# Causal mask of a 16-head self-attention: block rows inside the K=32 products and small triangle products, in place of 128x128 mask products

## Chip, cores, metric

The kernel runs on one core of a Trainium2 chip (trn2). The metric is the device time of one execution in microseconds (us).

## What is computed

A decoder of two layers over x of shape 64 x 128 x 128 (batch, position, model). The change touches only the first sublayer, a causal self-attention with 16 heads of width 8:

```python
x = x + _L0_attn_ref(_layernorm(x), W_dq, W_uq, W_dkv, W_uk, W_uv, W_o)

Q = ((x @ W_dq) @ W_uq).reshape(B, S, 16, 8)      # K, V alike
scores = jnp.einsum('bqhd,bkhd->bhqk', Q, K) / math.sqrt(8)
scores = jnp.where(causal, scores, -jnp.inf)
attn = jax.nn.softmax(scores, axis=-1)
out = jnp.einsum('bhqk,bkhd->bqhd', attn, V).reshape(B, S, 128)
return out @ W_o
```

Behind it come a cross-attention, a sparse mixture of 8 experts, a second self-attention, a second cross-attention and a dense mixture of 4 experts.

## The kernel before

The stage `self_attention` (L283 and on) works on one batch of 128 positions per step. It is software-pipelined by hand: in slot t every engine does, in a fixed order, its part of step t minus a lag (TURN, PROJECT, SCORE, SHIFT, WEIGH, VALUE, LAST, ADD). `run_slots` writes slots 0 to 23 and 64 to 83 out in full and runs slots 24 to 63 as a loop of 8 slots a turn, so it jumps back four times. Engines are tied by semaphores alone; each engine's order is the order of the code.

The 16 heads are 4 groups `g` of 4 heads. A group's 32 rows of `q` and of the block-diagonal `k_bd` lie in partitions 32g to 32g+31 (`strip(g)`), so a product of a group uses 32 rows of TensorE (K=32), and four groups can run side by side. Each group has a PSUM bank `ps_s[g]` of 128 x 512 (4 heads x 128). The groups form two pairs, (0, 1) and (2, 3).

Each batch's scores are made twice. First natural, queries in partitions (SCORE, products at L366): DVE takes each row's negated maximum over the keys (L547, two operations a pair, semaphore `max_done`). Then it splits those maxima in three bf16 parts (`pad`, L581 to L586), TensorE transposes `pad` (L399), and DVE spreads it to `m_bd` (L565, `shift_ready`). Two slots after SCORE they are made again turned, keys in partitions (WEIGH, products at L371), in the same banks, with the negated maxima added by a K=32 product of ones with `m_bd` (L357); ACT takes the exponentials (L445, `exp_done`), TensorE multiplies them by the values (VALUE, L390), and so on.

TensorE's slot is: `half(sl, 0)` (natural scores of pair 0, turned scores of pair 1), VALUE, two transposes (L399, L405), `half(sl, 1)` (natural of pair 1, turned of pair 0), then L413, the projections L420 to L422, L427 and L433. A half begins with the mask: a 128-row product of a bf16 identity with a 128 x 128 table of 0 and -1e30, over 512 columns, for each of its four banks (`masked`, L333): the natural ones wait for `exp_done`, the turned ones for `max_done`, one wait per bank:

```python
for n, g in enumerate(PAIRS[other]):
    pe.wait_ge(max_done[other], 2 * upto(sl, s + 2 + pair) - 1 + n)
    ...
    masked(ps_s[g], c.mask_k)
pe.wait_ge(shift_ready, s + 1)
```

DVE's slot is: statistics L557, maxima of pair 0 (L547), `m_bd` (L565), the residual (L571), maxima of pair 1 (L547), the split into `pad` (L581 to L586), L591, L596, L602. ACT's: exponentials of pair 1, L456, L461, L466, exponentials of pair 0, then `kT` (L476), q, v, xT. POOL builds `k_bd` from `kT` (L524) and small norm scalars. SP loads the tables (L267) and later streams zeros to memory.

## Time and profile before

| | |
|---|---|
| median of 3 runs | 3181.57 us (3179.53 to 3188.43) |
| the profiled execution's own time | 3173.24 us |
| its span | 3171.5 us |
| mean granted TensorE clock in it | 0.958 |
| this stage in the span | about 20 to 509 us |

The profiled execution is one run with its own time, 8.3 us under the median. PE is the matmul side of TensorE, PEld its weight loads, which overlap PE. A releaser is the instruction whose semaphore ended an idle time; "issue" means that nothing shown was waited for.

### The profile page before, as it was taken

The numbers are of one execution on the slowest core, as the hardware profiler recorded it, in microseconds if no ns is written. First come the engines' busy times: TensorE is split into PE (matmuls) and PEld (weight loads), VectorE is DVE, ScalarE is ACT, GpSimd is POOL, SyncE is SP. The second block draws the span as 40 slices with busy tenths as digits, with TensorE's granted clock in tenths as the row PEclk, the third lists the DMA queues.
The fourth block names the chain that finished last, engine by engine and source line by source line (L and its number), as shares of the span: only waits on it lengthen the run. The fifth ranks groups of instructions, "written<-read, shape, count | busy, mean of one in ns | idle before, by whom it ended". The sixth has DMA issues, their size and how long they took to land. (4 is left out here: it accounts for less than half of the span.)

```text
span 3171.5 us, 79074 instructions
## 1 busy us (share of the span) xinstructions
PE 2810.4 (89%) x26182; PEld 2315.9 (73%) x26183; DVE 2213.5 (70%) x4747; ACT 1914.9 (60%) x4303; POOL 1819.8 (57%) x2990
## 2 busy tenths in 40 slices
PE   6999997999999999499995999996789999999996
PEld 4666675888888888387774777774467777777775
DVE  4877885667666676445553999996878787878643
ACT  2555553666666666354442667674677777777762
POOL 3333333556666666425556777773667777777752
PEclk9999998999999999699997999997699999999998
DMA  5555563000000000122222000000000000000000
GB/s 151 156 143 157 157 169 107 2 5 13 14 11 13 13 12 15 68 69 74 74 74 68 1 0 0 0 0 1 1 1 5 8 5 8 5 8 5 8 5 10
DMA packets 205118, 129.51 MB, mean 41 GB/s; under 512 B 14256, under 2 KB 197528, under 8 KB 204184
## 3 DMA queue, kind: packets, MB, share of 16 engines
q1 hardware_dynamic: 196632, 108.60, 12.1%
q0 software_dynamic: 8192, 16.79, 1.7%
q8 instruction: 208, 3.41, 0.4%
q14 instruction: 86, 0.70, 0.1%
HBM read 34.85 MB, written 90.51 MB: 40 GB/s over the span
## 5 line engine op out<-in xcount | busy, mean ns | idle before, releaser
L445 ACT ACTIVATE a_e<-a_ps_s 128x512 f32<-128x512 f32 x256 | 138.9, 595 | 216.9 <-PE a_ps_s L371 216.9
L1575 POOL TENSOR_TENSOR a_qk<-a_qkv 128x2048 f32<-128x2048 f32 x64 | 235.3, 3676 | 57.8 <-ACT a_qkv L1550 53.6
L1508 PE MATMUL a_ps_s<-a_qk,w_ident 128*128 128x256 f32 x1024 | 236.7, 385 | 26.5 <-POOL a_qk L1575 26.4
L988 POOL TENSOR_TENSOR x_p<-x_p,x_rz 128x1232 f32<-128x1232 f32 x64 | 143.9, 2248 | 170.4 <-DVE x_rz L1097 170.4
L1508 PEld LDWEIGHTS a_ps_s<-a_qk,w_ident 128*128 128x128 f32 x1024 | 192.1, 192 | 55.9 <-issue 22.4
L524 POOL TENSOR_TENSOR a_k_bd<-a_kT,w_block 128x512 f32<-128x512 f32 x64 | 67.1, 1050 | 280.2 <-ACT a_kT L476 280.2
L1366 POOL DMA_INDIRECT f_yg<-f_rows_out,f_index x128 | 122.8, 959 | 177.7 <-DVE f_yo L1446 159.3
L547 DVE TENSOR_REDUCE a_nmax<-a_ps_s 128x4 f32<-128x512 f32 x256 | 164.0, 682 | 84.3 <-PE a_ps_s L366 84.3
L1557 ACT ACTIVATE a_r<-a_o,w_a_rows 128x128 f32<-128x128 f32 x512 | 220.8, 522 | 2.1 <-DVE a_o L1607 2.1
L2224 POOL TENSOR_TENSOR x_sq<-x_e 128x1232 f32<-128x1232 f32 x64 | 143.3, 2240 | 127.4 <-DVE x_t_sq L2383 127.3
L1104 DVE TENSOR_REDUCE x_top<-x_ps_s 128x16 f32<-128x1232 f32 x64 | 91.2, 1425 | 110.3 <-PE x_ps_s L728 110.3
L2102 ACT ACTIVATE x_pT<-x_ps_s 77x512 f32<-77x512 f32 x256 | 142.3, 590 | 34.6 <-PE x_ps_s L1979 34.6
L1526 PEld LDWEIGHTS a_ps_y<-w_a_o,a_r 128*128 128x128 f32 x1024 | 123.1, 195 | 54.6 <-issue 36.3
L865 ACT ACTIVATE x_uu_hi<-x_ps_u 128x308 fp32r<-128x308 f32 x256 | 101.7, 423 | 90.6 <-PE x_ps_u L728 90.4
L366 PE MATMUL a_ps_s<-a_k_bd,a_q 32*128 32x128 f32 x2048 | 154.1, 289 | 1.2 <-issue 1.2
L2205 POOL TENSOR_TENSOR x_d<-x_d,x_g 128x1232 f32<-128x1232 f32 x64 | 144.0, 2249 | 18.5 <-ACT x_g L2164 18.5
L1526 PE MATMUL a_ps_y<-w_a_o,a_r 128*128 128x128 f32 x1024 | 131.4, 283 | 24.4 <-DVE x L1622 24.2
L1979 PE MATMUL x_ps_s<-w_ident,x_d 128*77 128x128 f32 x1024 | 145.2, 280 | 7.7 <-DVE x_d L2366 7.6
L1597 DVE TENSOR_TENSOR a_ev<-a_ps_e,a_qkv 128x2048 f32<-128x2048 f32 x64 | 146.0, 2281 | 5.2 <-ACT a_ps_e L1564 4.1
L882 ACT ACTIVATE x_pT<-x_ps_s 77x512 f32<-77x512 f32 x256 | 140.0, 594 | 13.4 <-PE x_ps_s L786 12.0
L1979 PEld LDWEIGHTS x_ps_s<-w_ident,x_d 128*77 128x77 f32 x1024 | 124.4, 152 | 31.2 <-issue 22.1
L1019 POOL DMA_INDIRECT f_rows_in<-f_xr,f_where x120 | 121.1, 1009 | 39.2 <-issue 28.6
(588 smaller groups left out, 9755.6 us busy)
## 6 DMA issues: line engine op xcount, KB each, us to landing
f_rows_in<-a_zeros SPq DMA_DIRECT2D x31, 1088.0 KB, 5.4
f_rows_out<-a_zeros SPq DMA_DIRECT2D x31, 1088.0 KB, 10.2
f_xin<-f_rows_in SPq DMA_DIRECT2D x135, 64.0 KB
f_rows_out<-f_yo SPq DMA_DIRECT2D x135, 64.0 KB
out<-x SPq DMA_DIRECT2D x16, 256.0 KB
f_raw<-in_late_f SPq DMA_DIRECT2D x2, 1408.0 KB, 6.1
w_ctx<-in_ctx SPq DMA_DIRECT2D x1, 2464.0 KB
f_rows_in<-f_xr,f_where POOLq DMA_INDIRECT x128
```

Source lines behind the costliest of these rows:

```text
L366: nat = nc.tensor.matmul(ps_s[g][:, j * P:j * P + P], q[strip(g), u % 4, :], k_bd[strip(g), u % 4, j, :], start=False, stop=j == GROUP - 1)
L547: nc.vector.tensor_reduce(nmax[:, g, :], ps_s[g][:, :].rearrange("p (t k) -> p t k", t=GROUP), AX.X, ALU.max, negate=True).then_inc(max_do ...
L988: nc.gpsimd.tensor_tensor(wide, wide, rz[:, :].unsqueeze(2).broadcast_to([P, HEADS, K]), ALU.mult).then_inc(p_ready, 1)
L1508: ins = nc.tensor.matmul(ps_s[u % 2][:, 0:HEADS * HEADS], c.ident[:, :], qk[:, u % 2, k, :, :], start=k == 0, stop=k == HD - 1)
L1526: ins = nc.tensor.matmul(ps_y[:, 0:D], r[:, u % 2, k, :, :], c.w["a1_o"][:, k, :], start=k == 0, stop=k == HD - 1)
L1557: ins = nc.scalar.activation(r[:, u % 2, :, :, a], o[:, u % 2, :, :].rearrange("p h d -> p d h"), ACT.Copy, scale=c.w["a1_rows"][:, a:a + 1])
L1575: nc.gpsimd.tensor_tensor(qk[:, u % 2, :, :, :], qkv[:, u, 0, :, :].unsqueeze(3).broadcast_to(full), qkv[:, u, 1, :, :].unsqueeze(2).broad ...
L1597: nc.vector.tensor_tensor(ev[:, :, :, :], weights_of(u).unsqueeze(2).broadcast_to(n), qkv[:, u, 2, :, :].unsqueeze(1).broadcast_to(n), ALU ...
L1979: ins = nc.tensor.transpose(ps_s[0:K, r, j * P:j * P + P], d[:, spread % RING, r, j, :], c.ident[:, :])
L2102: nc.scalar.activation(pT[:, GROUP * r:GROUP * r + GROUP, :], ps_s[0:K, r, :].rearrange("p (j q) -> p j q", j=GROUP), ACT.Copy).then_inc(p ...
L2205: nc.gpsimd.tensor_tensor(wide, wide, g[:, a, b, :].unsqueeze(2).broadcast_to([P, HEADS, K]), ALU.mult).then_inc(dg_ready, 1)
L2224: nc.gpsimd.tensor_tensor(sq[:, :, :], e[:, s % 2, :, :], e[:, s % 2, :, :], ALU.mult).then_inc(sq_ready, 1)
```

## The change

The mask is written as products of 32 rows. Positions are cut in four blocks of 32. A whole block of later keys is masked by block rows: three rows of a strip hold a block indicator on one side and -1e30 for earlier blocks on the other. For the natural scores that is an own K=32 product per bank (`coarse_q`, `coarse_k`, new L348) over 512 columns, which now opens the bank. For the turned scores the same rows ride inside the shift product (`shift16` and rows of `pad` that the split never writes; `a0_block` lets them through in L565), which now opens the bank. The four diagonal blocks are masked by `causal_tiles` (new L334): per bank four K=32 products, `place16` (a shifted 32-row identity) with a 32 x 32 triangle repeated over 4 heads, 128 columns each. A half has four banks, so sixteen of them. The waits become one per pair: for the second operation of `exp_done` and of `max_done`; `shift_ready` is waited for ahead of `max_done`. The tables come as one load of 128 x 10 x 128 bf16 (320 KB) in place of four of 32 KB, and `a0_block` is a further load of 2 KB. DVE's one-time memset of `pad` becomes a copy.

```diff
--- before.py
+++ after.py
@@ -329,9 +329,10 @@
 
         @block.tensor
         def _(pe):
-            def masked(bank, mask):
-                nc.tensor.matmul(bank[:, :].rearrange("p (t k) -> p t k", t=GROUP), c.ident16[:, :],
-                                 mask[:, :].unsqueeze(1).broadcast_to([P, GROUP, P]), start=True, stop=False)
+            def causal_tiles(g, tri, n):
+
+                nc.tensor.matmul(ps_s[g].rearrange("p (t k) -> p t k", t=GROUP)[:, :, n * STRIP:n * STRIP + STRIP], c.place16[strip(g), n, :],
+                                 tri[strip(g), :].unsqueeze(1).broadcast_to([STRIP, GROUP, STRIP]), start=False, stop=False)
 
             def half(sl, pair):
 
@@ -339,22 +340,28 @@
                 scored, weighed = sl.step(SCORE), sl.step(WEIGH)
                 if scored:
                     s, u = scored
-                    for n, g in enumerate(PAIRS[pair]):
-                        if sl.fixed and s < 3 - pair:
-                            wait(pe, max_done[pair], 2 * s - 1 + n)
-                        else:
-                            pe.wait_ge(exp_done[pair], 2 * (s - 2 + pair) - 1 + n)
-                        masked(ps_s[g], c.mask_q)
+                    if sl.fixed and s < 3 - pair:
+                        wait(pe, max_done[pair], 2 * s)
+                    else:
+                        pe.wait_ge(exp_done[pair], 2 * (s - 2 + pair))
+                    for g in PAIRS[pair]:
+                        nc.tensor.matmul(ps_s[g][:, :].rearrange("p (t k) -> p t k", t=GROUP), c.coarse_q[strip(g), :],
+                                         c.coarse_k[strip(g), :].unsqueeze(1).broadcast_to([STRIP, GROUP, P]), start=True, stop=False)
                 if weighed:
                     s, u = weighed
-                    for n, g in enumerate(PAIRS[other]):
-                        pe.wait_ge(max_done[other], 2 * upto(sl, s + 2 + pair) - 1 + n)
-                        if sl.fixed and s + 2 + pair > B:
-                            pe.wait_ge(exp_done[other], 2 * s - 1 + n)
-                        masked(ps_s[g], c.mask_k)
                     pe.wait_ge(shift_ready, s + 1)
+                    pe.wait_ge(max_done[other], 2 * upto(sl, s + 2 + pair))
+                    if sl.fixed and s + 2 + pair > B:
+                        pe.wait_ge(exp_done[other], 2 * s)
                     for g in PAIRS[other]:
-                        nc.tensor.matmul(ps_s[g][:, :], c.ones16[strip(g), :], m_bd[strip(g), u % 2, :, :], start=False, stop=False)
+                        nc.tensor.matmul(ps_s[g][:, :], c.shift16[strip(g), :], m_bd[strip(g), u % 2, :, :], start=True, stop=False)
+                for n in range(GROUPS):
+                    if scored:
+                        for g in PAIRS[pair]:
+                            causal_tiles(g, c.tri_q, n)
+                    if weighed:
+                        for g in PAIRS[other]:
+                            causal_tiles(g, c.tri_k, n)
                 if scored:
                     s, u = scored
                     pe.wait_ge(q_ready, s + 1)
@@ -538,7 +545,7 @@
 
         @block.vector
         def _(dve):
-            nc.vector.memset(pad[:, :, :, :], 0.0)
+            nc.vector.tensor_copy(pad[:, :, :, :], c.a0_pad.rearrange("p (h r) -> p h r", r=HD).unsqueeze(1).broadcast_to([P, 2, HEADS, HD]))
 
             def maxima(at, pair):
                 s, u = at
@@ -563,7 +570,7 @@
                     wait(dve, sT_ps[0], s - 1)
                     wait(dve, sT_ps[1], s - 1)
                     nc.vector.tensor_tensor(m_bd[:, u % 2, :, :], ps_pad.unsqueeze(1).broadcast_to([P, GROUP, P]),
-                                            c.block[:, 0:GROUP].unsqueeze(2).broadcast_to([P, GROUP, P]),
+                                            c.a0_block[:, 0:GROUP].unsqueeze(2).broadcast_to([P, GROUP, P]),
                                             ALU.mult).then_inc(shift_ready, 1)
                 if at := sl.step(ADD):
                     s, u = at
@@ -2571,9 +2578,11 @@
                 c.w[name] = sb("w_" + name, shape, inp[name].dtype, life)
                 tiles[name] = c.w[name][(slice(None),) * len(shape)]
         keep = [(name, tiles[name]) for name in inp if name in tiles]
-        c.ident, c.ident16, c.ones_row = c.w["ident"], c.w["a0_ident16"], c.w["ones_row"]
-        c.mask_q, c.mask_k, c.ones16 = c.w["a0_mask_q"], c.w["a0_mask_k"], c.w["a0_ones16"]
-        c.block = c.w["block"]
+        c.ident, c.ones_row = c.w["ident"], c.w["ones_row"]
+        c.ident16, c.a0_pad, c.shift16, c.coarse_q, c.coarse_k = (c.w["a0_rows16"][:, n, :] for n in range(5))
+        c.place16 = c.w["a0_rows16"][:, 5:9, :]
+        c.tri_q, c.tri_k = (c.w["a0_rows16"][:, 9, n * STRIP:n * STRIP + STRIP] for n in range(2))
+        c.block, c.a0_block = c.w["block"], c.w["a0_block"]
         c.keys = inp["ctx"].shape[2]
         c.ctx = c.w["ctx"]
         c.rest = whole.enter_context(nc.semaphore("rest"))
@@ -2632,12 +2641,21 @@
     r = np.arange(P)
     strip = r % STRIP
     block = (strip[:, None] // HD == np.arange(GROUP)).astype(np.float32)
-    later = np.where(r[None, :] > r[:, None], MASKED, 0.0)
+    behind = strip - 2
+    coarse = (strip[:, None] == np.arange(3, 3 + GROUPS - 1)).any(axis=1)
+    low = MASKED * (r[None, :] // STRIP < behind[:, None]) * coarse[:, None]
+    at = (r[None, :] // STRIP == behind[:, None]) * coarse[:, None]
+    pad = np.zeros((P, GROUPS, GROUP, HD))
+    pad[:, :, 0, 3:3 + GROUPS - 1] = low[3:3 + GROUPS - 1].T[:, None, :]
+    place = [(strip[:, None] == r[None, :] - STRIP * n) for n in range(GROUPS)]
+    tri = np.zeros((P, P))
+    tri[:, 0:STRIP] = MASKED * (np.arange(STRIP)[None, :] > strip[:, None])
+    tri[:, STRIP:2 * STRIP] = MASKED * (strip[:, None] > np.arange(STRIP)[None, :])
+    rows = [np.eye(P), pad.reshape(P, P), (strip % HD < 3)[:, None] * ~coarse[:, None] + at, low, at] + place + [tri]
     return {
-        "ident": np.eye(P, dtype=np.float32), "a0_ident16": np.eye(P).astype(bf),
-        "a0_mask_q": later.astype(bf), "a0_mask_k": later.T.astype(bf), "a0_ones16": np.ones((P, P)).astype(bf),
+        "ident": np.eye(P, dtype=np.float32), "a0_rows16": np.stack(rows, axis=1).astype(bf),
         "tri4": triangles(4),
-        "block": block,
+        "block": block, "a0_block": np.maximum(block, coarse[:, None]).astype(np.float32),
         "ones_row": np.ones((1, P), np.float32),
     }
```

TensorE, the start of the second half of a slot (behind the transpose of `o`), before. A wait is named in brackets.

```order
L405 MATMUL a_ps_qkv<-w_ident,a_o 128x128 [waits a0_oT_ready,a0_v_ready,a0_o_ready]
L333 MATMUL a_ps_s<-w_a_mask_q,w_a_ident 128x512 [waits a0_exp_done1] x2
L333 MATMUL a_ps_s<-w_a_mask_k,w_a_ident 128x512 [waits a0_max_done0] x2
L357 MATMUL a_ps_s<-a_m_bd,w_a_ones 128x512 [waits a0_shift_ready]
L357 MATMUL a_ps_s<-a_m_bd,w_a_ones 128x512
L366 MATMUL a_ps_s<-a_k_bd,a_q 128x128 [waits a0_bd_ready,a0_q_ready]
L366 MATMUL a_ps_s<-a_k_bd,a_q 128x128
L371 MATMUL a_ps_s<-a_q,a_k_bd 128x128 x2
```

And in the changed kernel (`w_a_rows` is the new table):

```order
L412 MATMUL a_ps_qkv<-w_ident,a_o 128x128 [waits a0_oT_ready,a0_v_ready,a0_o_ready]
L348 MATMUL a_ps_s<-w_a_rows 128x512 [waits a0_exp_done1]
L348 MATMUL a_ps_s<-w_a_rows 128x512
L357 MATMUL a_ps_s<-a_m_bd,w_a_rows 128x512 [waits a0_max_done0,a0_shift_ready]
L357 MATMUL a_ps_s<-a_m_bd,w_a_rows 128x512
L334 MATMUL a_ps_s<-w_a_rows 128x4x32 x16
L373 MATMUL a_ps_s<-a_k_bd,a_q 128x128 [waits a0_bd_ready,a0_q_ready]
L373 MATMUL a_ps_s<-a_k_bd,a_q 128x128
L378 MATMUL a_ps_s<-a_q,a_k_bd 128x128 x2
```

Four 128-row products with their own waits are gone; the two openers of the natural banks, the two shift products and sixteen products of 128 columns stand ahead of the same L366 and L371 (now L373 and L378). The wait for `max_done` now stands at the shift product, beside `shift_ready`.

SP, the first loads, before:

```order
L265 DMA x<-in_x 128x4x128
L267 DMA w_ident<-in_ident 128x128
L267 DMA w_a_ident<-in_a_ident 128x128
L267 DMA w_a_mask_q<-in_a_mask_q 128x128
L267 DMA w_a_mask_k<-in_a_mask_k 128x128
L267 DMA w_a_ones<-in_a_ones 128x128
L267 DMA w_tri<-in_tri 128x32
L267 DMA w_block<-in_block 128x4
```

and in the changed kernel:

```order
L265 DMA x<-in_x 128x4x128
L267 DMA w_ident<-in_ident 128x128
L267 DMA w_a_rows<-in_a_rows 128x1280
L267 DMA w_tri<-in_tri 128x32
L267 DMA w_block<-in_block 128x4
L267 DMA w_a_block<-in_a_block 128x4
L267 DMA w_ones_row<-in_ones_row 1x128
```

Four loads became one, and `a_block` is new: two fewer ahead of the rest.

## Rows read from the trace of the kernel before

**Rows 1.** Page, part 1: busy time of each engine, whole span.

```profile
PE 2810.4 (89%) x26182; PEld 2315.9 (73%) x26183; DVE 2213.5 (70%) x4747; ACT 1914.9 (60%) x4303; POOL 1819.8 (57%) x2990
```

**Rows 2.** Stretches: from:to, length, busy (instructions) per engine, PE clock, DMA share, GB/s.

```profile
400.00:500.00 100.00, 99.49 (x1752) 72.24 (x1748) 82.64 (x222) 53.05 (x151) 32.33 (x72) 1.00 0.62 172
216.00:228.00 12.00, 11.54 (x153) 7.82 (x154) 5.04 (x12) 4.11 (x11) 3.73 (x15) 0.72 0.35 98
```

**Rows 3.** Waits of the stage, 36 to 506 us: in total, times, longest.

```profile
DVE a_nmax L547 <- PE a_ps_s L366: 84.3, 69, 15.9
...
PEld a_ps_s L333 <- DVE a_nmax L547: 25.9, 60, 0.5
```

**Rows 4.** Timeline of DVE, one slot: start, us, what, count, [idle before it, releaser].

```profile
299.09 1.29 DVE L547 TENSOR_REDUCE a_nmax<-a_ps_s 128x4 f32<-128x512 f32 x2 [0.80 <-PE a_ps_s L366]
...
300.94 0.93 DVE L581 CAST a_pad<-a_rest 128x16 bf16<-128x16 f32 x1
...
303.16 1.27 DVE L547 TENSOR_REDUCE a_nmax<-a_ps_s 128x4 f32<-128x512 f32 x2
...
306.03 1.29 DVE L547 TENSOR_REDUCE a_nmax<-a_ps_s 128x4 f32<-128x512 f32 x2 [0.80 <-PE a_ps_s L366]
```

**Rows 5.** Timeline of PEld (weight loads), second half of the slot.

```profile
304.49 0.10 PEld L333 LDWEIGHTS a_ps_s<-w_a_mask_k,w_a_ident 128*128 128x128 bf16 x1 [0.45 <-DVE a_nmax L547]
304.81 0.09 PEld L357 LDWEIGHTS a_ps_s<-a_m_bd,w_a_ones 32*128 32x128 bf16 x2 [0.23 <-issue]
304.82 0.19 PEld L366 LDWEIGHTS a_ps_s<-a_k_bd,a_q 32*128 32x128 f32 x2
```

**Rows 6.** Timeline of PE, second half of the slot.

```profile
304.81 0.39 PE L357 MATMUL a_ps_s<-a_m_bd,w_a_ones 32*128 32x512 bf16 x2
...
305.04 0.27 PE L371 MATMUL a_ps_s<-a_q,a_k_bd 32*128 32x128 f32 x2
...
305.70 0.27 PE L366 MATMUL a_ps_s<-a_k_bd,a_q 32*128 32x128 f32 x1
...
305.71 0.38 PE L371 MATMUL a_ps_s<-a_q,a_k_bd 32*128 32x128 f32 x3
```

**Rows 7.** Timeline of ACT, then POOL, around the DVE row at 300.94.

```profile
299.21 1.08 ACT L445 ACTIVATE a_e<-a_ps_s 128x512 f32<-128x512 f32 x2 [1.48 <-PE a_ps_s L371]
300.23 0.28 ACT L476 ACTIVATE a_kT<-a_ps_qkv 128x128 f32<-128x128 f32 x1
...
300.73 1.08 POOL L524 TENSOR_TENSOR a_k_bd<-a_kT,w_block 128x512 f32<-128x512 f32 x1 [5.03 <-ACT a_kT L476]
```

**Rows 8.** Timeline of DVE, last scored slot, where no a_k_bd is built.

```profile
497.35 0.20 DVE L581 CAST a_pad<-a_rest 128x16 bf16<-128x16 f32 x1
```

**Rows 9.** Timeline of PE, small products of another stage.

```profile
686.12 0.23 PE L851 MATMUL x_ps_misc<-x_mask,w_x_all 128*128 128x32 bf16 x3
686.20 0.24 PE L854 MATMUL x_ps_misc<-x_mask,w_x_all 128*128 128x8 bf16 x4
```

**Rows 10.** Timeline, another stage: a DVE operation and the load behind a separate wait.

```profile
527.34 0.48 DVE L1035 TENSOR_TENSOR x_uu_lo<-x_ps_u,x_uu_hi 128x308 fp32r<-128x308 f32 x1 [4.41 <-ACT x_uu_hi L865]
...
527.94 0.29 PEld L726 LDWEIGHTS x_ps_u<-x_keys_hi,x_a_hi 128*128 128x128 f32 x1 [0.78 <-issue]
```

**Rows 11.** Timeline of PEld, DVE and PE at loop turns.

```profile
155.79 0.13 PEld L333 LDWEIGHTS a_ps_s<-w_a_mask_q,w_a_ident 128*128 128x128 bf16 x2 [2.90 <-issue]
...
159.36 0.69 DVE L547 TENSOR_REDUCE a_nmax<-a_ps_s 128x4 f32<-128x512 f32 x1 [3.12 <-PE a_ps_s L366]
...
218.13 0.42 PE L366 MATMUL a_ps_s<-a_k_bd,a_q 32*128 32x128 f32 x1
219.00 0.36 PE L366 MATMUL a_ps_s<-a_k_bd,a_q 32*128 32x128 f32 x1 [0.46 <-issue]
```

**Rows 12.** Timeline of SP's queue (SPq) at the start.

```profile
2.22 0.43 SPq L267 DMA_DIRECT2D w_a_mask_q<-in_a_mask_q  x1
2.70 0.43 SPq L267 DMA_DIRECT2D w_a_mask_k<-in_a_mask_k  x1
```

## Prediction

> **What bounds the kernel now.** I read five views. The page gives PE 2810.4 us of a 3171.5 us span [rows 1], which would make TensorE the bound. The change, though, lies in one stage of some 490 us, so the stretch table comes next: from 400 to 500 us PE is busy 99.49 of 100, DVE 82.64 [rows 2]. A busy PE is a modelled one, so this doesn't say what a shorter TensorE slot would be worth. The waits of the stage do: DVE waits 84.3 us for the natural scores (L366), 69 times, and TensorE's load waits 25.9 us, 60 times, for DVE's maxima [rows 3]. Each waits for the other once a slot: a loop between two engines, and its length is the slot.
>
> The timeline shows it. DVE's maxima of pair 1 start at 299.09 and again at 306.03, so the slot is 6.94 us, with one idle time of 0.80 in it [rows 4]. All the rest DVE works or is held. The maxima of pair 0 end at 303.16 + 1.27 = 304.43 [rows 4]. Call this time T. At 304.49 TensorE's load of the last mask product of the second half is released; the load of the shift product follows at 304.81 [rows 5]; the last natural product ends at 305.70 + 0.27 = 305.98 [rows 6], and DVE goes on at 306.03 [rows 4]. So T to DVE's next start is 1.60 us, and this is TensorE's only share in the loop. The rest of its slot is ahead of T or behind 306, beside DVE's work.
>
> A second branch of the loop: the last turned product ends at 305.71 + 0.38 = 306.09 [rows 6]. The slot before shows what hangs on it: exponentials at 299.21 for 1.08, `kT` at 300.23, and POOL's `k_bd` from 300.73 for 1.08 [rows 7]. DVE's cast at 300.94 takes 0.93 us [rows 4], where the same cast takes 0.20 without a `k_bd` beside it [rows 8]; it ends as `k_bd` ends (301.87 and 301.81). So DVE's small operations are held to the end of `k_bd`, which goes back to the last turned product. That product is the one that sets the slot: natural scores a little earlier or later meet the same hold.
>
> **What TensorE saves, and where it lies.** A product of 512 bf16 columns holds its strip for about 0.22 us (L357 at 304.81, L371 of its strips at 305.04 [rows 6]). A half loses four full-array mask products in series, 4 x 0.22 = 0.87. The two natural openers use other strips than the shift products and run beside them: nothing added. The sixteen triangles are four per strip, strips side by side, 128 columns or 0.055 each: 4 x 0.055 = 0.22. Behind them the first fp32 load of a strip is exposed: an fp32 load takes 0.19 and a bf16 one 0.09 [rows 5], so it streams about 0.10, of which the last triangle hides 0.055: 0.05. Saved are 0.87 - 0.27 = 0.60 a half, 1.2 a slot, some 75 us of TensorE's time in 63 slots. It lies ahead of T: TensorE comes to the second half's shift product over 1 us sooner and waits there for DVE.
>
> **What changes behind T.** Removed: from 304.49 to 304.81, one mask product and the change from 128-row to 32-row products: -0.33 [rows 5]. The change of form isn't gone but made earlier, by the natural openers. Added: the triangles, 0.22, and the exposed load, 0.05, since both now stand behind `max_done`, and nothing of them can run ahead of it. Also the wait itself. Until now `max_done` was on the weight load: 0.06 from DVE's end to the load (304.43, 304.49). Now L357 has two waits and the first in the code is `shift_ready`; the second becomes an instruction of its own. Another stage prices that: DVE ends at 527.34 + 0.48 = 527.82 and the load starts at 527.94, 0.12 [rows 10]: +0.06. Behind it queue the triangles and all L373 and L378, for which DVE and ACT wait. Sum for the turned branch: -0.33 + 0.22 + 0.05 + 0.06 = 0.00; I take +0.02 for the gaps of a few ns between triangles, times 60 slots: **+1 us**.
>
> The bounds of this term. The triangles' spacing in four strips is not in this trace. Below: four fp32 products start within 0.01 to 0.02 us and the next four 0.11 later, so strips hardly hinder each other; with triangles fully packed and the load hidden it is -0.05 a slot, -3 us. Above: the small products at 686.12 start 0.025 to 0.027 apart (three from 686.12, the next at 686.20) although 32 columns need half of that [rows 9]. At 0.025 each sixteen take 0.40: +0.18 a slot, +11 us, more if DVE meets `k_bd` an operation earlier. Those are whole-array loads, one behind the other, and mine are in four strips, so I stand near the first end.
>
> The Trainium skill speaks against this change here: "TensorEngine Tiling (Array Packing)", section Instruction Overhead, says that each matmul costs some 60 cycles whatever its width and warns of small ones, which is 0.025 us. The rows of the products of 8 and 32 columns agree with it; by that rule the sixteen would cost 0.40 and the sum would be 3191, not 3180.
>
> **First half of a slot.** It needs the maxima of pair 1 and saves 0.60 too, but DVE is then in its small operations and comes to the natural scores of pair 0 only at 303.16 [rows 4], when they have long been there (no idle time stands at that row). Nothing gained. The `exp_done` wait for both operations of a pair costs nothing: at 299.21 + 1.08 = 300.29 they are done [rows 7], before TensorE gets there.
>
> **Loop turns.** Four times the loop jumps back, TensorE's loads pause 2.90 us and DVE idles 3.12 [rows 11]. There TensorE is late, so its first half is on the path and shorter masks can give 0.6 to 1.3 each. But some 70 instructions behind the jump it pauses again in two of the four turns (218.13 to 219.00, "issue" [rows 11]), as if instructions came late; the new half has 28 more (14 loads, 14 products), uses them up faster, and has more left behind that pause: up to +1 each. Between -5 and +4 us, I take **-2**.
>
> **Start and end.** Two fewer loads are issued ahead of the others, 0.47 apart (2.22, 2.70 [rows 12]); 200 KB more are moved. Between -1 and +1, I take **-0.5**. `a0_block` for `block` in L565 has the same shape: 0. The copy for a memset on `pad` is once, beside POOL's start: 0. The later stages are the same work: 0.
>
> **Sum.** 1 - 2 - 0.5 = -1.5 us. Against the profiled execution's own 3173.24 (span 3171.5) that is 3171.7. Its time is 8.3 under the median of the runs, 3181.57, which stands for the kernel: 3181.57 - 1.5 = **3180 us**. A difference of 0.3%, 9.5 us, is about what a measurement of this kernel tells from none.
>
> **Rivals.**
> - *Small products too dense (slower).* The triangles go 0.025 apart. Turned scores then end 0.18 later a slot, natural ones, whose loads queue behind all sixteen, up to 0.2 later, so that the hold by `k_bd` catches DVE one small operation sooner (0.24 more). It decides from 0.16 a slot on (9.5 / 60). For: [rows 9]. Against: the starts of four strips within 0.02. Time: +11 to +25, 3193 to 3206, say 3197. Chance 0.17.
> - *TensorE slows for its new idle time (slower).* It idles over 1 us a slot in one piece. From 216 to 228, behind the pause at a turn, the granted clock is 0.72 [rows 2], so partly at 1.2 GHz instead of 2.4. At 1.2 the 1.5 us behind T double; ten such slots more are +15, 3196. Against: from 400 to 500 the clock is 1.00 [rows 2] although loads wait up to 0.45 a slot for DVE [rows 5]. Chance 0.07.
> - *TensorE is the bound after all (faster).* If the natural scores came sooner by all that TensorE saves, DVE's idle 0.80 would go: 60 x 0.8 = 48 us, 3133. For: PE at 99%. Against: what DVE waits for is released by DVE itself 1.60 us before. Chance 0.05.
> - *The loop gets a little shorter (faster).* Strips independent, all four turns at their best, DVE's small operations fall better around `k_bd`: -0.1 to -0.2 a slot and -5, so -11 to -17, 3168. Chance 0.11.
>
> **How the numbers follow.** The forecast, within 9.5 us of before, keeps 0.60. Faster is 0.05 + 0.11 = 0.16, slower 0.17 + 0.07 = 0.24. The range leaves out the bound case (0.05) and the upper parts of the two slower ones (about 0.1): 3167 to 3199.
>
> **What would show it.** After the change: the slot stays at 6.9 to 7.0 us. DVE's idle time ahead of the maxima of pair 1 stays near 0.8 (0.7 to 0.8 if strips are independent, 1.0 if products are 0.025 apart). PE's busy time in the stage falls, and the load of L357 waits about 1 us a slot for DVE (L554), where 25.9 us stood in all before. DVE's operation beside `k_bd` still takes 0.93. Starts of L334 in one strip stand 0.055 to 0.06 apart. The forecast is wrong if DVE's idle time shrinks below 0.5, if `k_bd` no longer meets DVE's small operations, or if the clock of the stage falls under 0.9.

## The result and the profile after

The changed kernel takes 3215.35 us (median of 4 runs, 3205.61 to 3220.97), the kernel before 3180.55 in the same session (4 runs, 3176.11 to 3188.43): a ratio of 1.0103, 95% interval [1.0071, 1.0136]. It is slower by 1%, where 3180 and no change were forecast. The profiled execution of the kernel after is the fastest of its four (3205.61 us), so what the two traces below account for is a difference of 32.3 us of span (3171.5 and 3203.8), not the 34.8 of the medians.

Page, part 1, of the kernel after (span 3203.8 us), against [rows 1]; then its stretches of [rows 2] and one of the later x0 stage, with the same columns:

```profile
PE 2786.1 (87%) x27974; PEld 2342.9 (73%) x27975; DVE 2218.4 (69%) x4747; ACT 1921.6 (60%) x4303; POOL 1818.8 (57%) x2990
```

```profile
400.00:500.00 100.00, 89.95 (x2091) 73.46 (x2091) 80.58 (x210) 52.72 (x150) 32.83 (x71) 0.97 0.57 158
850.00:950.00 100.00, 94.23 (x815) 84.09 (x815) 65.13 (x137) 61.96 (x133) 63.30 (x105) 0.98 0.03 12
```

TensorE runs 1792 products more and is busy less. In the stretch it falls from 99.49 to 89.95 of 100, and the whole didn't get faster by it. The slot itself is what was forecast. Timeline of DVE, one slot of the kernel after:

```profile
299.84 1.27 DVE L554 TENSOR_REDUCE a_nmax<-a_ps_s 128x4 f32<-128x512 f32 x2
...
302.61 1.29 DVE L554 TENSOR_REDUCE a_nmax<-a_ps_s 128x4 f32<-128x512 f32 x2 [0.71 <-PE a_ps_s L373]
...
304.46 0.94 DVE L588 CAST a_pad<-a_rest 128x16 bf16<-128x16 f32 x1
...
306.69 1.27 DVE L554 TENSOR_REDUCE a_nmax<-a_ps_s 128x4 f32<-128x512 f32 x2
...
309.46 0.69 DVE L554 TENSOR_REDUCE a_nmax<-a_ps_s 128x4 f32<-128x512 f32 x1 [0.71 <-PE a_ps_s L373]
```

The slot is 309.46 - 302.61 = 6.85 us (6.94 before), the idle time 0.71 (0.80), and the cast beside `k_bd` still takes 0.94. Over slots 7 to 60 of both traces the undisturbed ones (up to 8% over the median) have a mean of 6.91 us, against 6.97 before. TensorE's saved time stands as waiting ahead of its shift product. Loads of the same slot, then the waits of the stage (36 to 506 us: in total, times, longest), against [rows 3]:

```profile
301.16 0.09 PEld L357 LDWEIGHTS a_ps_s<-a_m_bd,w_a_rows 32*128 32x128 bf16 x2 [0.88 <-DVE a_nmax L554]
```

```profile
DVE a_nmax L554 <- PE a_ps_s L373: 89.3, 72, 13.0
PEld a_ps_s L357 <- DVE a_nmax L554: 33.1, 36, 1.1
...
PEld a_ps_s L348 <- issue: 17.2, 10, 4.5
...
PE a_ps_s L348 <- issue: 14.7, 4, 4.2
...
PEld a_ps_s L378 <- issue: 7.0, 4, 2.3
PE a_ps_s L378 <- issue: 5.4, 3, 2.1
```

The rows that matter are those "<- issue": TensorE waits for nothing that the profile shows, in a few long pieces. Before, the largest were 13.1 us in 10 (L333). By stage, from the first instruction on a tile of each (before, after): a0 from the first `a_ps_s` to the first `x_bank` 477.6 and 491.0 us (+13.4); then wide_weights and x0 to the first `f_w_hi` 809.9 and 827.4 (+17.5), though that code is unchanged; the rest +1.5. The x0 stage loses it at one place of its loop, which jumps back four times. Timeline of PE behind one of these jumps (a branch at 967.69):

```profile
971.87 0.40 PE L733 MATMUL x_ps_s<-x_uu_hi,x_x_hi 128*128 128x308 f32 x1 [1.59 <-issue]
972.11 0.31 PE L734 MATMUL x_ps_s<-x_uu_lo,x_x_hi 128*128 128x308 f32 x1
972.25 0.31 PE L735 MATMUL x_ps_s<-x_uu_hi,x_x_lo 128*128 128x308 f32 x1
974.35 0.62 PE L733 MATMUL x_ps_s<-x_uu_hi,x_x_hi 128*128 128x308 f32 x1 [1.79 <-issue]
```

There is a pause at the jump, three products, and a second pause. The kernel before has the first kind alone (1.58 us ahead of the product at 861.30, at its first x0 jump).

The second pause is 2.0 to 2.3 us without a weight load, 8.7 us in the four turns, about half of what the stage lost. The other half is TensorE's clock behind it. One pass of the loop, from branch to branch, in the kernel before, in the kernel after, and in x0_shifted_12 (below), where the second pause is gone, with the columns of [rows 2]:

```profile
951.80:1046.50 94.70, 90.61 (x803) 80.75 (x802) 64.82 (x136) 60.55 (x131) 61.51 (x105) 1.00 0.03 13
```

```profile
967.70:1066.60 98.90, 93.28 (x803) 83.18 (x801) 64.97 (x136) 61.12 (x131) 61.48 (x105) 0.97 0.03 12
```

```profile
959.80:1053.70 93.90, 90.55 (x802) 80.67 (x801) 64.86 (x136) 60.92 (x131) 61.64 (x105) 1.00 0.03 11
```

The same 803 products keep PE busy for 93.28 us in place of 90.61. Over the four passes that is 9.8 us more of busy time in 16.4 us more of length (395.0 for 378.6), and the trace of the kernel after has 23.8 us of them at half the clock (1.2 GHz), each stretch beginning in a second pause or just over 1 us behind it. The kernel before and x0_shifted_12 have none there.

**What the pauses have in common.** I numbered the instructions of TensorE's program (a product is two, load and product; a wait of its own is one) and put them beside the trace. All pauses of this second kind stand at numbers that leave the same rest when divided by 256, up to ten instructions. In the a0 stage of the kernel after TensorE stops 9 behind number 1758, 9 and 3 behind 4830 (in the first and the last pass of the loop), and 10 behind 6110, 6878 and 9182, and in the x0 stage at 14046; each of these is 222 + a multiple of 256. The page counts 223 transfers of the instruction queue (208 before), and each one of them in the trace is 16384 bytes, which is 256 instructions of 64 bytes. From 400 to 510 us, in straight code, there are 19 of them for 18 blocks of 256 instructions of TensorE. I call 222 + 256n an **edge**. The x0 loop starts 60 instructions ahead of an edge in the kernel before and 11 ahead of one in the kernel after, because TensorE's program in front of it has grown by 1841 instructions, which is 7 x 256 + 49.

The Trainium skill says this in "Runtime: NRT & Kernel Launch", section Instruction fetch mechanics: instructions come in 16 KiB blocks of 256, fetched one after the other ahead of use, and a taken branch out of the blocks held forces a fetch before work goes on. The trace agrees with both. The section also calls the crossing of a block's end mostly hidden; the trace shows up to 2.4 us there.

### The profile page after: what moved, and what is told of

Its sections match the earlier page's. It is cut to its first block and busy times, and to the rows that moved or that the text cites. A ratio compares the mean times of both kernels' runs of the same rounds, so it can differ in the third digit from the quotient of the medians.

```text
span 3203.8 us, 82733 instructions
## 1 busy us (share of the span) xinstructions
PE 2786.1 (87%) x27974; PEld 2342.9 (73%) x27975; DVE 2218.4 (69%) x4747; ACT 1921.6 (60%) x4303; POOL 1818.8 (57%) x2990
## 5 line engine op out<-in xcount | busy, mean ns | idle before, releaser
L373 PE MATMUL a_ps_s<-a_k_bd,a_q 32*128 32x128 f32 x2048 | 156.2, 293 | 1.8 <-issue 1.8
L378 PE MATMUL a_ps_s<-a_q,a_k_bd 32*128 32x128 f32 x2048 | 151.2, 286 | 5.4 <-issue 5.4
L1533 PE MATMUL a_ps_y<-w_a_o,a_r 128*128 128x128 f32 x1024 | 131.6, 283 | 24.2 <-DVE x L1629 23.7
```

The source lines that it names most:

```text
L373: nat = nc.tensor.matmul(ps_s[g][:, j * P:j * P + P], q[strip(g), u % 4, :], k_bd[strip(g), u % 4, j, :], start=False, stop=j == GROUP - 1)
L378: turned = nc.tensor.matmul(ps_s[g][:, j * P:j * P + P], k_bd[strip(g), u % 4, j, :], q[strip(g), u % 4, :], start=False, stop=j == GROUP - 1)
L1533: ins = nc.tensor.matmul(ps_y[:, 0:D], r[:, u % 2, k, :, :], c.w["a1_o"][:, k, :], start=k == 0, stop=k == HD - 1)
```

## Experiments

Sessions on the chip differ: the kernel before took 3180.6, 3146.6, 3148.5, 3146.2 and 3182.7 us in the five groups of runs below, most of it in the experts' stage (859 to 866 us from `f_w_hi` to `f1w`, or 836 to 839, whatever the kernel). The x0 stage differs too: 797.8 us in hybrid_masks and 807.6 in hybrid_max_first, for the same x0 code. So ratios to the kernel before of the same group are compared, and stage times of the traces. Theory A: instructions come late. Rival B: chance, or the clock. Rival D: triangles and waits behind `max_done`. "Excess" is the time of slots 7 to 60 over the same number of median slots. Some expectations count the x0 stage from 13 us earlier: their 823 and 840 us are the 809.9 and 827.4 here.

### Is it the place of the code?

x0_shifted_back. Tiny products move the x0 loop of the kernel after to 59 instructions ahead of an edge:

```diff
+            for n in range(104):
+                nc.tensor.matmul(spare[:, 0:8], c.ident16[:, :], c.ident16[:, 0:8], start=True, stop=True)
```

> The changed kernel with 104 tiny products (8 columns, into an unused bank; 208 instructions) at the end of TensorE's part of wide_weights, where TensorE waits for other engines. The x0 loop then starts in TensorE's program 8 x 256 instructions behind its place before the change, up to one instruction. Theory A (instructions arrive in pieces of 256, and the loss of the later stage comes from where its loop lies against the edges of the pieces): the second pause behind each of the four jumps of the x0 loop (2.1 to 2.4 us, L735 to L733) goes, the x0 stage (first bank product to the first f_w_hi operation) falls from 840.4 to about 823 us, and the median falls from 3215 to about 3198. The a0 stage stays 13 us longer than before the change. Rival B (the x0 loss is chance or the clock's doing): the stage stays at 840 and the pauses stay. Rival C (the added products cost time): the stage gets 3 us longer.

1.0052 [1.0036, 1.0069], x0 stage 813.0 us. The second pauses are gone. The a0 stage, the same code, is 497.3 us (491.0 in the trace of after, 486.8 in that of x0_shifted_12 below), so a0 varies by some 10 us between executions. Rival B falls as the first cause, since the pauses go with the place of the code; the added products cost nothing that shows.

x0_shifted_before. The same with `range(24)` in the kernel before:

> The kernel before with 24 such tiny products (48 instructions) at the same place: the x0 loop starts 12 instructions ahead of an edge of 256, as in the changed kernel, instead of 60. Theory A: a second pause of 2.1 to 2.4 us comes behind each of the four jumps of the x0 loop, the stage grows from 823 to about 839 us, the median from 3181 to about 3196. Rival B (chance or clock): stage 823, median 3181 within 9. Nothing of the change itself is in this kernel, so a slower time can't be due to masks.

1.0060 [1.0043, 1.0077], x0 stage 827.0 (809.9), 20.4 us of its four passes at half the clock. 48 instructions that nothing needs make the kernel before 0.6% slower, by the mechanism forecast. Timeline of PE behind a jump (branch at 961.60), where the kernel before has one pause:

```profile
966.02 0.40 PE L729 MATMUL x_ps_s<-x_uu_hi,x_x_hi 128*128 128x308 f32 x1 [1.83 <-issue]
966.26 0.30 PE L730 MATMUL x_ps_s<-x_uu_lo,x_x_hi 128*128 128x308 f32 x1
966.40 0.30 PE L731 MATMUL x_ps_s<-x_uu_hi,x_x_lo 128*128 128x308 f32 x1
969.04 0.40 PE L729 MATMUL x_ps_s<-x_uu_hi,x_x_hi 128*128 128x308 f32 x1 [2.34 <-issue]
```

x0_shifted_12. Only `range(6)` in the kernel after:

> The changed kernel with only 6 tiny products (12 instructions) in wide_weights. The x0 loop then starts 255 instructions ahead of an edge of 256 (11 in the changed kernel) and ends 245 behind one, 11 ahead of the next. Theory A with the start of the loop alone deciding: the four second pauses of 2.1 to 2.4 us go, x0 stage 827 to about 810 us or 806 on the faster chip, ratio 1.0050 against 1.0103 of the changed kernel. If the end counts as well, because TensorE's queue reads past the jump over the edge (as in a0_shifted, whose loop ends 240 behind an edge and still paused 3.4 to 3.9 us at its jumps): the pause at each jump grows from 1.4 to 3 or more, and half or less of the gain is left, ratio 1.007 to 1.009.

1.0034 [1.0020, 1.0048], x0 stage 807.2 us. It is better than I expected, below the kernel before (809.9), and the "if the end counts" branch is wrong here: a loop end 11 ahead of an edge costs nothing. All pauses at the jumps are gone. Waits of PE from 850 to 1270 us, the kernel after, then this one:

```profile
PE x_ps_s L733 <- issue: 14.1, 8, 2.1
PE x_ps_u L733 <- DVE x_uu_lo L1042: 7.8, 12, 0.7
```

```profile
PE x_ps_u L736 <- DVE x_uu_lo L1045: 11.4, 16, 0.9
PE x_ps_u L736 <- POOL x_keys_lo L990: 1.9, 8, 0.3
```

Twelve instructions more are worth 20 us of the stage, pauses and clock together.

### What is lost in the a0 stage?

The kernels from here on keep the x0 loop clear of the second pause (a0_shifted by the same products that move its a0 loop, the others by tiny products in wide_weights). So a kernel with the new mask is to be compared with x0_shifted_back (1.0052), not with 1.0103.

before_more_instructions. The kernel before with as many products a half as the changed one, and the same place of its a0 loop:

```diff
-                nc.tensor.matmul(bank[:, :].rearrange("p (t k) -> p t k", t=GROUP), c.ident16[:, :],
-                                 mask[:, :].unsqueeze(1).broadcast_to([P, GROUP, P]), start=True, stop=False)
+                for n in range(GROUP):
+                    nc.tensor.matmul(bank[:, n * P:n * P + P], c.ident16[:, :], mask[:, :], start=n == 0, stop=False)
```

> The kernel before with each mask product cut into four of 128 columns and each shift product into two: 36 products a half, as in the changed kernel, for about the same time of the array; tiny products ahead of the a0 loop put its start at the same place against the edges of 256 as in the changed kernel (132 instructions ahead of an edge, the end 53 behind one), and more in wide_weights keep the x0 loop where it was before. Theory A: the a0 stage grows by 6 to 15 us (pauses at the jumps from 2.8 to about 4.2 us, some pauses of 1 to 2 us at edges), x0 stays at 823, median about 3190. Rival D (the loss of the a0 stage comes from the triangles or from the waits behind max_done): a0 stage as before within 3 us, median 3181.

1.0032 [1.0022, 1.0042], a0 stage 484.6 (+7.0), excess 24.7 us (16.7 before, 28.0 after). The pauses at the four jumps are 3.9, 4.1, 3.9 and 4.2 us, where the kernel before has 2.6 to 3.0 and the one after 2.5, 4.3, 4.4 and 4.2. The old mask with the new number and place of instructions has over half of the a0 loss: by the runs 0.32% of the 0.52% of x0_shifted_back. The stage times of single traces say less, as the kernel before's own a0 code took 477.6 us in one trace and 482.1 in x0_shifted_before.

a0_shifted. `range(90)` of the tiny products ahead of the a0 slots of the kernel after:

> The changed kernel with 90 tiny products (180 instructions) ahead of the a0 slots, where TensorE waits for the first norm from 19 to 30 us: the a0 loop then starts 208 instructions ahead of an edge of 256 (132 before) and ends 240 behind one (60 before); the x0 loop starts 87 ahead of one (11 before). Theory A: pauses at the a0 jumps fall from 4.2 to at most 2.8 us, the a0 stage loses 6 to 12 of its 13 us of extra time, the x0 stage its 17; median 3184 to 3192. Rival D (triangles or waits cost the 13 us): a0 stage stays 13 longer, only x0 gains, median 3198. Rival B: nothing changes, 3215.

1.0025 [1.0015, 1.0036]. The x0 stage is 809.7, as expected. The a0 stage is 488.6, 2.4 us under the trace of after and 8.7 under x0_shifted_back. The runs are the better measure: the median, 3188.87, lies in the 3184 to 3192 forecast, 9.3 us under x0_shifted_back (3198.22, same session), of which 3.3 are its shorter x0 stage. So some 6 us were gained. But the pauses at the jumps are 3.4 to 3.9, not at most 2.8, so the gain didn't come the way I said, and the pause at a jump can't be reckoned from the start of the loop alone.

no_triangles. The kernel after without the `causal_tiles` calls, which leaves out the mask inside the diagonal blocks:

> The changed kernel without its triangle products (the mask inside the diagonal blocks of 32 is left out), x0 loop in its place of before. The a0 loop starts 132 ahead of an edge and ends 60 behind one, as in the changed kernel, with 1986 instructions instead of 2498. My sum of the prediction (triangles 0.22 us a half, of it all behind the maxima in the second half): steady slot 6.93 - 0.22 - 0.05 = 6.66, unless the hold by k_bd keeps it; rival B (small products 0.025 us apart): 6.93 - 0.40 = 6.53. Theory A: the pauses at the jumps are set by the place of the loop's end, so they stay near 4.2 us; if they are set by the number of instructions they fall to 2.8. Median against x0_shifted_back (3198): -15 to -20 with the pauses unchanged.

0.9988 [0.9978, 0.9998]. The pauses at the jumps stay long (slots of 11.0 to 11.3 us), though a turn of the loop has 1986 instructions in place of 2498, so place has more to do with them than number. Timeline of DVE, the maxima of one slot:

```profile
303.81 1.27 DVE L547 TENSOR_REDUCE a_nmax<-a_ps_s 128x4 f32<-128x512 f32 x2
...
306.44 1.29 DVE L547 TENSOR_REDUCE a_nmax<-a_ps_s 128x4 f32<-128x512 f32 x2 [0.57 <-PE a_ps_s L366]
```

The mean slot is 6.77 against 6.91: the triangles cost 0.14 us, half of what I expected (6.66). Of the 20 us between this kernel and x0_shifted_back that is some 9; excess falls too, to 21.2 from 33.3. From the end of the maxima of pair 0 to DVE's next start it is 1.36 us without and 1.50 with them, to the end of the last turned product 1.34 and 1.62. So they take 0.28 of the turned branch, near the 0.27 of my sum, but only 0.14 of the natural branch, which DVE waits for and which the slot follows. Two at a time they start 0.056 us apart (301.239, 301.295, 301.350 in the trace of after), in the 0.055 to 0.06 forecast. At 0.025 us each they would have cost 0.40.

after_no_jumps and before_no_jumps. TensorE's slots written out:

```diff
-            run_slots(pe, slot, B, LAG, RING)
+            for t in range(B + LAG):
+                slot(Slot(t, t % RING, B, True, RING))
```

> The changed kernel with TensorE's slots of the a0 stage all written out, no loop on TensorE (the other engines keep theirs), and 17 tiny products in wide_weights so that the x0 loop stands against the edges of 256 instructions as in the kernel before. Theory A (the a0 loss is instructions coming late, most of it at the four jumps): the slots at the jumps lose their 24 us over the steady slot of 6.93, a few late pieces stay (0 to 8 us); against x0_shifted_back (3198) the median is 3172 to 3184. Rival D (the 13 us are triangles or waits, and the long slots at the jumps have another cause, such as the scalars of a batch of eight): a0 stage as in the changed kernel within 4 us, median 3195 to 3201. Rival H (straight code is fetched worse than a loop): slower than 3198.

> The kernel before with TensorE's slots of the a0 stage written out in the same way, and 78 tiny products in wide_weights to keep the x0 loop in its place. Theory A: the slots at the jumps lose 18 us over the steady slot of 6.97, median 3160 to 3170 against 3180.5. With both kernels free of jumps what is left between them is the change itself: steady slots 0.06 us shorter, 62 times, against 28 more instructions a half, so the changed one -4 to +6 us. Rival D: the changed one 10 to 15 us slower here too.

1.0000 [0.9990, 1.0009] and 0.9970 [0.9957, 0.9982]. a0 stages 477.9 and 464.8. The changed kernel is 0.3%, some 9 us, slower than the other, beyond the -4 to +6 forecast and close to the 10 to 15 of rival D, so this pair alone doesn't decide. The slots do. In the kernel before none from 7 to 60 is disturbed any more (excess -0.4 us). In the changed one 10.3 are left: slots 16, 30, 40, 44 and 54 take 8.8 to 10.5 us, though TensorE jumps nowhere, and slot 6 takes 10.2. Waits from 36 to 500 us, first before_no_jumps, then after_no_jumps:

```profile
PEld a_ps_s L366 <- issue: 1.7, 2, 0.8
...
PEld a_ps_s L333 <- issue: 0.8, 3, 0.3
```

```profile
PEld a_ps_s L378 <- issue: 8.5, 5, 2.1
PE a_ps_s L373 <- issue: 5.8, 4, 1.9
```

The changed kernel crosses an edge every 6.0 us, the one before every 7.0 (medians of 90 to 480 us), and of the changed one's pieces five landed 0.3 to 0.7 us behind the crossing; none did before, where the nearest was 1.5 ahead. TensorE goes on 1.3 to 1.6 us behind the landing of those five, a piece that lands 0.65 us ahead still costs 0.84, and one 1.15 ahead nothing that shows. A written-out program is the better one for both: over the a0 slots of the changed kernel 20.4 us are at half the clock, where the loop had 37.4 (47.7 in x0_shifted_back), and in the kernel before none, where the loop had 13.6.

### Why do pieces of straight code come late?

clears_unpaced, the kernel after (x0 loop shifted back) with the zero-filling transfers of the a0 stage no longer waiting for `x_done`; clears_halved, with its two transfers of 1088 KB in turn, one per slot, instead of both every second slot:

```diff
-                sp.wait_ge(x_done, 2 * n + 1)
-                for rows in (c.f0_x, c.f0_y):
+                for m, rows in enumerate((c.f0_x, c.f0_y)):
+                    sp.wait_ge(x_done, 2 * n + 1 + m)
```

> The changed kernel, x0 loop in its place of before (as x0_shifted_back, 3198), with the zero-filling transfers of the a0 stage no longer paced by the slots: they come one behind the other and are through in the first 240 us or so. Theory G (a piece of instructions is asked for too late when those transfers occupy the DMA engines): behind their end no slot but those at the jumps is over 7.5 us, the jumps' pauses there fall from 4.2 towards 2.8 us, and more slots of the first part are long. Sum: a0 stage -8 to +8. Rival (the lateness has nothing to do with the traffic): pauses of 4.2 at all four jumps and some long slots between 400 and 500 us as before (398, 428, 499 us).

> The changed kernel, x0 loop in its place of before (as x0_shifted_back, 1.0052 of before), with the two zero-filling transfers of 1088 KB that went out together every second slot of the a0 stage going out one per slot: the same bytes in bursts half as long. Theory G (a piece of instructions is asked for late when it falls into a burst): the late pieces away from the jumps (8 to 14 us in the changed kernel) shrink to 0 to 4 us, the jumps' pauses stay between 2.8 and 4.2. Against x0_shifted_back -5 to -12 us, ratio to before 1.001 to 1.004. Rival (the share of traffic counts, not the length of a burst): within 3 us of 1.0052.

> after_no_jumps (1.0000 of before) with the zero-filling transfers halved in the same way. Theory G: its five long slots (10.3 us over the steady slot) go or are under 3 us in sum: ratio to before 0.9965 to 0.9985. Rival: stays at 1.0000.

> before_no_jumps (0.9970 of before; no long slot left) with the zero-filling transfers halved. Theory G: nothing left to gain, 0.996 to 0.998. With after_no_jumps_halved it gives the worth of the change where no instruction comes late: steady slots 6.91 against 6.97 us, 62 times, so the changed one is 2 to 6 us faster; by rival D (triangles and waits cost the 13 us) it would be over 8 us slower.

Unpaced: 1.0108 [1.0072, 1.0143], a0 stage 516.6, far outside my -8 to +8. Stretches of it, with and without the traffic (the last three columns are the granted clock, DMA share and GB/s):

```profile
100.00:280.00 180.00, 136.60 (x2950) 110.93 (x2944) 114.70 (x313) 77.75 (x220) 48.01 (x110) 0.89 1.04 283
300.00:480.00 180.00, 157.64 (x3709) 127.96 (x3701) 146.88 (x392) 97.93 (x275) 63.23 (x143) 0.97 0.01 3
```

Under the traffic 15 slots are over 7.5 us, those of two jumps 17.6; behind it only those of the last two jumps, at 10.0 and 10.2 instead of 11.4 and 11.1, and the slot after the last. The traffic delays the pieces, and 58.0 us of the stage are at half the clock. But the halved bursts made it worse (1.0107 [1.0089, 1.0125]; 1.0016 [1.0006, 1.0027] without jumps; the kernel before 0.9957 [0.9944, 0.9971], no slot disturbed), where I expected a gain. The median slot itself grew, from 6.93 to 7.18 us, with pauses of 0.5 to 0.9 at many edges, and the pauses at the jumps from 4.2 to 6.7. The mistake was the unit. One transfer of 1088 KB occupies the DMA engines for 3.85 us (burst length in clears_halved; 7.75 for the pairs). Of 66 instruction transfers of clears_halved between 90 and 460 us, 45 start within 0.5 us of the end of a burst and 5 inside one, though bursts fill half of the time. With pairs, in the kernel before, all 23 that start inside a burst start over 5 us into it, that is behind the first transfer's 3.85; in the kernel after 3 of 19 start 1.5 to 1.7 us into one. My reading is that a piece mostly waits for the bulk transfer under way, up to its whole 3.85 us, and that parting a pair shortens no transfer and makes more ends to wait for. The trace shows when a piece's transfer starts, not when it is asked for, so the wait is inferred. Smaller transfers are the remedy that would follow; I didn't try them.

### What is the change worth where instructions come in time?

All kernels of this group have TensorE's a0 and x0 slots written out and half of the zero-filling moved to the x0 stage. before_written_out is the kernel before so, but with all zero-filling still in a0, one transfer per slot.

> before_no_jumps_halved with TensorE's slots of the x0 stage written out too (8 slots a loop, five passes, four jumps). Theory A: at each of the four jumps TensorE pauses 1.1 to 1.7 us now, so the x0 stage loses up to 6 us: ratio to before 0.994 to 0.997. If the pause is hidden behind other engines: as before_no_jumps_halved.

> The changed kernel with TensorE's slots of a0 and x0 written out (no jumps) and only f0_x zero-filled in the a0 stage (1088 KB every second slot instead of 2176); f0_y is zero-filled in the x0 stage from a zero tensor in DRAM. Theory G2 (a piece of 256 instructions is asked for late while bulk transfers occupy the DMA engines, and the changed kernel needs a piece every 5.5 to 6.5 us instead of 8 to 13): the long slots of after_no_jumps (10.3 us) fall to 2 to 6, the a0 stage from 478 to 470 to 474; ratio to before 0.9945 to 0.9965. Rival (lateness independent of traffic): a0 478, ratio 0.9978. Rival (the traffic moved to x0 makes that late): x0 stage over 800 us.

> The same for the kernel before (before_written_out was 0.9930): no long slot was left there, so 0.992 to 0.994, a0 stage 462. The difference to after_light_traffic is what the change costs where few instructions come late: theory A and G2 +0.000 to +0.003 with 0.06 us a slot gained and some late pieces left; rival D (triangles and waits) over +0.004 without any long slot in the trace.

> after_light_traffic with the wait for max_done written ahead of the one for shift_ready, so that the other order of attached and separate wait results. My sum priced the separate instruction at 0.06 us a slot in the second half (0.12 us from the end of DVE's maxima to the load against 0.06): if so the steady slot falls by 0.06 and the time by 3 to 4 us (0.001). Rival: both waits cost the same, within 1 us in the steady slots.

> after_light_traffic, but only the turned products get the new mask (coarse rows and triangles); the natural ones get the mask product of 128x128 again: 28 products a half instead of 36, all the 1.1 us ahead of the shift product having room for two of 0.22 us. Theory: steady slot as in after_light_traffic within 0.03 (the way behind max_done is the same), fewer instructions, so fewer late pieces: 1 to 4 us faster than after_light_traffic. Rival (TensorE's saved time ahead of max_done is worth something): slot 0.1 or more longer.

> hybrid_masks (0.9931) with the wait for max_done written ahead of the one for shift_ready, as in after_light_max_first, where the steady slot fell from 7.02 to 6.91 us. Theory: slot 6.91, a0 stage 456 to 458 us, at most one late piece: ratio to before 0.9895 to 0.9905, the fastest of all and 1 to 5 us under before_light_traffic (0.9913). Rival (the fast slot of after_light_max_first needs the short natural masks): slot 6.95 or more, 0.991 or above.

The last two have the old mask for the natural products; those "max_first" this edit:

```diff
-                    pe.wait_ge(shift_ready, s + 1)
                     pe.wait_ge(max_done[other], 2 * upto(sl, s + 2 + pair))
                     if sl.fixed and s + 2 + pair > B:
                         pe.wait_ge(exp_done[other], 2 * s)
+                    pe.wait_ge(shift_ready, s + 1)
```

| kernel | ratio to before | a0 stage, us | mean slot | excess |
|---|---|---|---|---|
| before_written_out | 0.9930 [0.9916, 0.9943] | 462.4 | 6.97 | 0.0 |
| before_light_traffic | 0.9913 [0.9899, 0.9927] | 459.4 | 6.96 | -0.3 |
| after_light_traffic | 0.9934 [0.9921, 0.9948] | 465.2 | 7.02 | 2.5 |
| after_light_max_first | 0.9908 [0.9893, 0.9924] | 459.7 | 6.91 | 3.4 |
| hybrid_masks | 0.9931 [0.9918, 0.9945] | 462.9 | 7.00 | 0.9 |
| hybrid_max_first | 0.9913 [0.9893, 0.9932] | 456.7 | 6.91 | 0.7 |

With the traffic halved the excess of the written-out changed kernel falls from 10.3 to 2.5 us. Its steady slot surprised me: 7.02, longer than the 6.91 of the same code in a loop. The order of waits explains it. Timeline of PEld at the shift product, after_light_traffic (maxima of pair 0 end at 305.62 + 1.27 = 306.89), then after_light_max_first (302.53 + 1.27 = 303.80):

```profile
307.01 0.12 PEld L357 LDWEIGHTS a_ps_s<-a_m_bd,w_a_rows 32*128 32x128 bf16 x2 [1.10 <-issue]
```

```profile
303.86 0.09 PEld L357 LDWEIGHTS a_ps_s<-a_m_bd,w_a_rows 32*128 32x128 bf16 x2 [1.04 <-DVE a_nmax L556]
303.86 0.23 PEld L334 LDWEIGHTS a_ps_s<-w_a_rows 32*128 32x128 bf16 x10
```

Where `max_done` is an instruction of its own the load comes 0.12 us behind DVE, where it sits on the load 0.06. In the loop of the changed kernel `shift_ready` had been taken up by a register instruction, so `max_done` sat on the load. The two loads also start 0.03 us apart in the first and together in the second. In these two slots that is the whole gain: DVE's idle time ahead of the maxima of pair 1 falls from 0.80 to 0.71. The mean slot gains 0.11.

With few late instructions and the waits in the better order the new mask can't be told from the old one: 0.9908 and 0.9913. In the order in which it was written it is 0.2% behind (0.9934), within what I expected, though the intervals touch. The hybrid with the better order has the shortest a0 stage of all, 456.7 us, and the slot of 6.91 that I expected; in the whole time its 0.9913 missed my 0.9895 to 0.9905, and it can't be told from the other two. All three are about 0.9% faster than the kernel before; 0.7 of that the kernel before has from being written out (before_written_out).

## Why the prediction was wrong

- **What bounds the slot: right.** DVE and TensorE release each other, TensorE's share behind T is 1.50 us after (1.59 before), and all that TensorE saves ahead of T became waiting (load of L357, 0.88 a slot). The bound case (3133) didn't come.
- **What changes behind T: near, -0.06 us a slot measured for +0.02.** The triangles cost the turned branch 0.28 for the 0.27 reckoned (no_triangles). The +0.06 for a wait of its own was right as a price (0.12 against 0.06, after_light_traffic) but not due in the loop, where the wait for `shift_ready` went into a register instruction; without it my sum is -0.06. Which branch sets the slot I had wrong: the turned one gained 0.04 (1.66 to 1.62), the natural one 0.09, and without the triangles the slot follows the natural one (0.14), not the turned one (0.28). *Small products too dense* is out. By the rule of the Trainium skill's "TensorEngine Tiling (Array Packing)", section Instruction Overhead, the sixteen would have cost 0.40; for triangles in four strips the trace doesn't agree.
- **Loop turns: the first step that failed.** I took -2 us, range -5 to +4. The four turns with the slot behind each took 8 slots + 18.5 us before and 8 slots + 24.2 after: +5.7. I had seen the second pause at 219.00 [rows 11], called it instructions coming late, and priced it by the number of added instructions. What decides is the place against edges of 256 (no_triangles, with fewer instructions at the same place, pauses as long), and I didn't look for one.
- **No term at all for straight code.** Slots 6, 48 and 52 are 1.3, 3.1 and 1.8 us longer than the steady one and the last scored slot 3.0 longer than before: +9 us. I had no term for an edge away from a jump. It takes more instructions a slot and the bulk transfers together (excess 10.3 us in after_no_jumps, 2.5 in after_light_traffic, -0.4 in before_no_jumps).
- **"The later stages are the same work: 0": the costliest step.** It was the same work at another place, +17.5 us, half of the loss. x0_shifted_before gives it to the kernel before by 48 idle instructions, x0_shifted_12 takes it away by 12. About half of it is the pauses and half the lower clock behind them.
- **Rival of the clock: wrong in its condition, and yet the clock carries part of the loss.** The short idle time of every slot doesn't lower it: where no long pause is (after_light_traffic, 200 to 400 us) it is 1.00 with TensorE idle in every slot. The long pauses do. Over the a0 slots 13.6 us are at half the clock before and 37.4 after, over the four x0 passes none and 23.8. I priced late instructions by their pause alone. How much of the a0 loss is clock no run separates; the slot behind a jump takes 8.0 to 8.4 us there in place of 6.9.

Sum by steps in the trace of after: turns +5.7, straight code +9, steady slots -3, which makes 12 of the a0 stage's 13.4; x0 17.5 (pauses and clock); the rest of the span +1.5. Open is what decides the pause at a jump where the loop is well placed at its start: a0_shifted still pauses 3.4 to 3.9 us, x0_shifted_12 not at all, and the four a0 jumps of x0_shifted_back, the same code at the same place as in the kernel after, pause 4.4, 2.3, 4.5 and 2.2 us.

## What to carry to other kernels

A change in the number of an engine's instructions moves all code behind it, so reckon, beside the work, where the loops land against blocks of 256 instructions, and before believing any 1% test it with a few idle instructions in front. On an engine that runs 256 instructions in some 6 us, "<- issue" pauses of 1 us and more are the sign, and each costs its own length and the lower clock behind it. Write the slots out, keep bulk traffic away from such a stage (shorter transfers may do, untested), and put the wait that comes last first in the code, where it ended up on the load here. Time saved on an engine ahead of what it waits for is worth nothing, and what it costs in instructions isn't free.

## What the runs showed that I hadn't expected

- Behind an x0 jump the target's piece comes first, and the transfer of the next one starts 3.4 to 3.5 us later (968.62 and 972.12 in the kernel after; 952.84 and 956.26 before). What stands between decides: 60 instructions last until it has landed, 11 don't.
- At the a0 jumps of the kernel after two pieces are fetched at once, 0.7 to 1.7 us behind the branch, and take 1.6 to 2.3 us each (216.31 and 216.44: 1.8) instead of 0.9 to 1.6. The loop ends 60 instructions behind an edge, so one of them may be the piece that follows it in the program, which isn't needed at a jump back. No run separates that.
- An instruction transfer of 16 KB seems to wait for a bulk transfer that is under way, up to 3.85 us (45 of 66 start just behind a burst, 5 inside one). A loop of 2042 instructions, eight pieces, is fetched anew in every pass: 9 to 11 transfers stand between two of its jumps.
- Long pauses lower TensorE's clock behind them: the x0 stage lost as much by 23.8 us at half the clock as by the pauses.
- Written-out code was 0.3% faster than the loop (before_no_jumps), and there, from slot 17 to 47, nearly all slots of the same place in eight agree within 10 ns.
